# GpSimd takes the whole low-half subtraction in the two head attentions, VectorE makes both halves of their outputs

## What is computed

```python
qh = (q @ Wq).reshape(B, N, H, 8); kh, vh = the same of the context
attn = softmax(einsum(qh, kh) * 8 ** -0.5)      # 16 heads x 56 queries = 896 columns, 1500 keys
out = einsum(attn, vh).reshape(B, N, 128) @ Wo
x = x + out
```

## Time and profile before

| | us |
|---|---|
| median of 3 runs | 3920.25 (3919.48 to 3924.01) |
| the profiled execution's own time | 3916.58 |
| span of its trace | 3914.4 |
| first head, first to last start of L594 | 1222.8 to 1892.7 |
| second head, first to last start of L594 | 1973.6 to 2642.3 |

### The profile page before, as it was taken

The page is one execution under the profiler, slowest core; times in us unless marked ns, Lnnn a source line. Parts: engine busy times, 40 slices in busy tenths (PEclk is TensorE's granted clock), DMA queues, the critical chain, the costliest instruction groups (busy, mean ns, idle before and its releaser), DMA issues.

```text
span 3914.4 us, 126748 instructions
## 1 busy us (share of the span) xinstructions
PE 3608.5 (92%) x51275; PEld 2774.8 (71%) x51275; DVE 3262.6 (83%) x6773; ACT 2699.6 (69%) x5391; POOL 2060.1 (53%) x2087
## 2 busy tenths in 40 slices
PE   6999999989987999999799999996996999999987
PEld 4777777766654777777567777774774677777775
DVE  6988888858887999999799999987555888888863
ACT  4777777756655888888478888872442677777752
POOL 3666666668973555555545555661003444455451
PEclk7999999989998999999799999997997999999998
DMA  5333333215545555565166555530001212222100
GB/s 146 110 107 103 105 108 108 81 56 155 152 116 142 153 152 142 153 160 136 35 160 155 153 147 148 153 98 21 1 1 34 65 56 60 59 62 57 56 22 16
DMA packets 224592, 385.85 MB, mean 99 GB/s; under 512 B 71848, under 2 KB 127800, under 8 KB 222648
## 3 DMA queue, kind: packets, MB, share of 16 engines
q1 hardware_dynamic: 223560, 377.69, 35.5%
q10 hardware_dynamic: 448, 0.06, 0.0%
HBM read 252.30 MB, written 103.08 MB: 91 GB/s over the span
## 4 chain that ended last, share of the span: by engine, by line
PE 68%; DVE 17%; DMA 5%; issue 3%; SPq 3%; ACT 2%; POOL 1%; DVEq 0%; POOLq 0%; ACTq 0%
PE ps L208 64%; DVE wst L1177 5%; DMA big<-headq 4%; DVE wst L1160 2%; DVE wst L1157 2%; DVE relu L1157 1%; SPq L946 1%; DVE cTs L999 1%; DVE xn L188 1%; SPq L967 1%; PE ps L2006 1%; PE ps L712 1%; PE ps L275 1%; POOL wst L594 1%; ACT wst L1097 0%
## 5 line engine op out<-in xcount | busy, mean ns | idle before, releaser
L594 POOL TENSOR_TENSOR wst<-wst 125x448 bf16<-125x448 f32 (+2 forms) x1536 | 1356.6, 883 | 1235.5 <-ACT wst L792 639.5
L208 PEld LDWEIGHTS ps<-cx,wst 125*128 125x128 bf16 x32256 | 1196.2, 98 | 220.6 <-POOL wst L594 12.6
L208 PE MATMUL ps<-cx,wst 125*128 125x65 bf16 (+1 forms) x32256 | 1243.1, 193 | 10.5 <-POOL wst L594 9.3
L792 ACT ACTIVATE wst<-ps 125x448 f32<-125x448 f32 x1536 | 752.7, 544 | 275.2 <-PE ps L208 273.4
L1131 ACT ACTIVATE wst<-ps 125x448 f32<-125x448 f32 x1536 | 751.0, 544 | 93.1 <-PE ps L208 82.0
L208 PE MATMUL ps<-big,cx 128*125 128x448 bf16 (+1 forms) x3072 | 714.5, 354 | 0.9 <-DMA big<-topT 0.9
L848 DVE TENSOR_TENSOR wst<-wst 125x640 bf16<-125x640 f32 (+1 forms) x768 | 646.7, 842 | 21.9 <-ACT wst L792 21.7
L1177 DVE TENSOR_TENSOR wst<-wst 125x448 bf16<-125x448 f32 x768 | 627.1, 817 | 18.4 <-ACT wst L1131 18.1
L208 PE MATMUL ps<-big 97*128 97x224 bf16 (+2 forms) x3872 | 586.2, 280 | 5.5 <-POOL big L1430 2.1
L208 PEld LDWEIGHTS ps<-big,cx 128*125 128x125 bf16 (+1 forms) x3072 | 418.4, 137 | 142.2 <-DMA big<-topT 1.7
L208 PEld LDWEIGHTS ps<-big 97*128 97x128 bf16 (+2 forms) x3872 | 372.5, 98 | 183.9 <-ACT wst L1131 9.7
(11 more groups left out here) (268 smaller groups left out, 5232.6 us busy)
## 6 DMA issues: line engine op xcount, KB each, us to landing
big<-headk SPq DMA_DIRECT2D x192, 375.0 KB, 5.6
headk<-cTs SPq DMA_DIRECT2D x128, 375.0 KB, 4.6
cx<-ctxT SPq DMA_DIRECT2D x96, 375.0 KB, 10.0
cx<-ctxN SPq DMA_DIRECT2D x64, 377.9 KB
cx<-in_ctxN SPq DMA_DIRECT2D x64, 375.0 KB
big<-big SPq DMA_DIRECT2D x384, 56.0 KB, 2.6
big<-headq SPq DMA_DIRECT2D x64, 224.0 KB, 7.1
ctxN<-cx SPq DMA_DIRECT2D x32, 377.9 KB
```

What stands on the lines that cost most here:

```text
L208: return t.matmul(o, l, r, start=start, stop=stop, skip_group_check=True)
L594: g.tensor_tensor(pl[r][0:KP, at:], pf[r][0:KP, at:], pf[r][0:KP, at:].bitcast(BF16)[:, 1::2], ALU.subtract).then_inc(s["plp"], 1)
L792: e.activation(pf[T % 3][0:KP, cols], bank(2 + n2 % 3, 448)[0:KP], ACT.Exp, scale=scale).then_inc(s["ev"], 1)
```

## The change

In heads, `SPLIT` becomes 0: GpSimd subtracts all 896 columns in one instruction and VectorE none, and GpSimd no longer waits for `pl`. PE waits for GpSimd at block 0. The output of an image is made out of PSUM by VectorE alone, the high half in one instruction and the low half in seven of 64 columns (multiply by the reciprocal, subtract the high half). ScalarE's copy and GpSimd's subtraction for it go away in heads, and PE, before it writes an `acc` again, waits for both halves instead of for `raw`. Attentions 0 and 3 keep their split; only the counts that their semaphores wait for are renumbered.

```diff
--- before.py
+++ after.py
@@ -18,7 +18,7 @@
 NJ = HQ // 128
 HB = 16
 QB = 6
-SPLIT = (640, 448, 448, 512)
+SPLIT = (640, 0, 0, 512)
 NT = KT * B
 EPS = 1e-5
 TWICE = 6
@@ -589,12 +589,10 @@
                 if 0 <= T - 1 < NT:
                     r, at = (T - 1) % 3, SPLIT[ci]
                     w.wait_ge(s["ev"], evacuated(ci, T - 1) + 2)
-                    if ci in (1, 2):
-                        w.wait_ge(s["pl"], NT * ci + T)
                     g.tensor_tensor(pl[r][0:KP, at:], pf[r][0:KP, at:], pf[r][0:KP, at:].bitcast(BF16)[:, 1::2],
                                     ALU.subtract).then_inc(s["plp"], 1)
                     w.wait_ge(s["plp"], NT * ci + T)
-                if 0 <= (k := due(T, KT + 6)) < B - 1:
+                if 0 <= (k := due(T, KT + 6)) < (B - 1 if ci in (0, 3) else 0):
                     kb = B * ci + k
                     w.wait_ge(s["fp"], 2 * kb + 1)
                     g.tensor_tensor(O[:, k % HB, :, C:], raw[k % 2], O[:, k % HB, :, 0:C], ALU.subtract).then_inc(s["fp"], 1)
@@ -604,12 +602,13 @@
             k, i = divmod(T, KT)
             r, kb = T % 3, B * ci + k
             ph, o, of = pf[r][0:KP, :].bitcast(BF16)[:, 1::2], acc[k % 2], cnb[k % 3]
-            w.wait_ge(s["pl"], NT * ci + T + 1)
+            if SPLIT[ci]:
+                w.wait_ge(s["pl"], (NT if ci else 0) + T + 1)
             wait_values(w, ci, k)
             if kb >= 2:
-                w.wait_ge(s["fc"], kb - 1)
+                w.wait_ge(s["fp"], 2 * (kb - 1))
             for j in range(NJ):
-                if 128 * j == SPLIT[ci] or j == 3 and SPLIT[ci] == 448:
+                if 128 * j == SPLIT[ci]:
                     w.wait_ge(s["plp"], NT * ci + T + 1)
                 cols, at = slice(128 * j, 128 * j + 128), 65 * j
                 mm(t, o[:, at:at + 64], ph[:, cols], of[:, i, 65:129], i == 0 and j == 0, False)
@@ -625,6 +624,17 @@
             if k >= 2:
                 w.wait_ge(s["fp"], 2 * (kb - 1))
             w.wait_ge(s["rd"], kb + 1)
+            if not SPLIT[ci]:
+                if k >= HB:
+                    w.wait_ge(s["otr"], kb - HB + 1)
+                hi, lo = O[:, k % HB, :, 0:C], O[:, k % HB, :, C:]
+                v.tensor_tensor(hi, o[:, :, 0:C], per_row(rden[u][:, :], C), ALU.mult).then_inc(s["fp"], 1)
+                w.wait_ge(s["fp"], 2 * kb + 1)
+                for j in range(NJ):
+                    n = v.scalar_tensor_tensor(out=lo[:, j, :], in0=o[:, j, 0:C], scalar=rden[u][:, j:j + 1], in1=hi[:, j, :],
+                                               op0=ALU.mult, op1=ALU.subtract)
+                n.then_inc(s["fp"], 1)
+                return
             v.tensor_tensor(raw[u], o[:, :, 0:C], per_row(rden[u][:, :], C), ALU.mult).then_inc(s["fc"], 1)
             if k == B - 1:
                 w.wait_ge(s["fp"], 2 * kb + 1)
@@ -632,7 +642,7 @@
 
         def act_values(e, w, ci, k):
             kb = B * ci + k
-            w.wait_ge(s["fc"], kb + 1)
+            w.wait_ge(s["fc"], (B if ci else 0) + k + 1)
             w.wait_ge(s["fp"], 2 * kb)
             if k >= HB:
                 w.wait_ge(s["otr"], kb - HB + 1)
@@ -1105,8 +1115,6 @@
                     w.wait_ge(s[f"tops_{k % 2}"], 16 * (ci * B // 2 + k // 2))
                     e.activation(topT[k % 2][:, :], bank(2 + n2 % 3, 128)[0:NJ], ACT.Copy).then_inc(s["ev"], 1)
                     n2 += 1
-                if (k := due(T, KT + 4)) >= 0:
-                    act_values(e, w, ci, k)
                 what, p, k = head_slot(T)
                 if what == "keys split":
                     act_keys(e, w, ci, p, k)
@@ -1170,12 +1178,6 @@
             for c in range(3):
                 dve_keys(v, w, ci, 0, c)
             for T in range(-26, HEAD_LAST):
-                if 0 <= T - 1 < NT:
-                    r = (T - 1) % 3
-                    w.wait_ge(s["ev"], evacuated(ci, T - 1) + 1)
-                    to = SPLIT[ci]
-                    v.tensor_tensor(pl[r][0:KP, 0:to], pf[r][0:KP, 0:to], pf[r][0:KP, 0:to].bitcast(BF16)[:, 1::2],
-                                    ALU.subtract).then_inc(s["pl"], 1)
                 if (k := due(T, -18)) >= 0:
                     keys(k)
                 if (k := due(T, -5)) >= 0:
```

## The result

The changed kernel takes 3967.87 us (median of 4 runs, 3964.79 to 3968.99), the kernel before took 3919.86 in the same comparison (4 runs, 3918.67 to 3924.01): a ratio of 1.0115, 95% interval 1.0103 to 1.0127. It is slower by 48 us; 27 were forecast. The profiled execution took 3968.99.

What follows compares the result with a forecast made beforehand. The prediction took VectorE to set the heads' pace, about 1.75 us a step, passing to GpSimd at 1.757. Terms 7.2 + 1.0 + 11 + 4 + 4 = +27 us on 3920.25 gave 3947, range 3926 to 3984.

Steps and rivals of the forecast that it cites:

- the case that was held most likely: Heads: GpSimd sets the pace, with short dry spells; 3935 to 3965 us, chance 0.68.
- VectorE's pace passes to GpSimd's: Heads: the step goes from VectorE's 1.749 and 1.746 us to GpSimd's 1.757; +7.2 us.
- The dearer subtraction: Rival: GpSimd's 896-column subtraction takes 1.87 us, a step 1.95; +153 us, 4073, chance 0.05.
- The output's dry spell: PE's 16 output matmuls in two steps running make GpSimd stand 0.31 to 0.4 us, 30 times; +11 us.
- The transposed block: Its copy on ScalarE and a relu stand before the exponentials; GpSimd loses 0.12 us, 30 times; +4 us.
- The key difference: VectorE's L1165, once an image, waits for GpSimd, then holds its next subtraction 0.06 us, 62 times; +4 us.
- VectorE's block: Seven 64-column output instructions an image, 1.35 us, delay VectorE's next maximum by about 1.3 us; costed at nothing.
- The ends: Both ends of a head: last subtraction 0.75 us longer, first starts some 0.25 earlier; +1.0 us for two heads.
- The faster rival: Wide subtraction under 1.67 us, so PE sets the pace at 1.68 a step: 52 us less, 3868, chance 0.06.
- The costly exclusion: Rival: VectorE's key difference waits for GpSimd, the product is late; 1 us an image, +60, 3980, chance 0.07.

Runs made afterwards that it cites:

- The splits: Changed kernel with the outputs' low halves spread over four steps and VectorE given back 128 or 256 of 896 columns: 3945.45 and 3992.98 us.

## Why the prediction was right, and what it mis-sized

The time, 3967.87, lies 3 us above the 3935 to 3965 of the case that was held most likely, and inside the range of 3926 to 3984.

- *VectorE's pace passes to GpSimd's.* Right. L592 has a median of 1.682 us (1.679 forecast), 0.08 between two, 1.76 a step (1.757). Worth +9.6 us, +7.2 forecast; with a clear way in front of it (the kernel with more run-ahead and spread outputs) it gives 3935, and the kernel with GpSimd whole and the outputs before shows the same 1.76 without any dry spell. The dearer subtraction, 1.87 us at its bound, did not come; nor did the estimate by the Trainium skill's GPSIMD Engine Reference, section 3.1 (about 2.6 cycles an element, 1.94 us).
- *The output's dry spell*, 0.31 to 0.4 us: measured 0.35 us. Right, +10.
- *The transposed block*, 0.12 us: 0.09 as a rule, but up to 1.4 in four periods of the second head, mostly where the queries' transfer is late; +6 for +4. The prediction saw that transfer only as a ground for its costly rival.
- *The key difference*, 0.06 us: L592's longest is 1756 ns against 1680, about 0.07, as forecast +4. That it would wait up to 1.7 us for GpSimd was wrong here: its median is 410 ns, its longest 1884, and only 3 of 64 are over 600. At 1491.91 it starts just where GpSimd's step ends. With GpSimd at 768 columns the same instruction lasts 1594 ns in the mean.
- *VectorE's block*: this is the step that failed. It was costed at nothing because "PE's product meets it two slots (3.5 us) later". Its own length was right (1.35 us for the seven, 1.44 in the trace). But the reciprocal and the high half stand before them in the same block, so the maximum comes 2.0 us late (1485.7 to 1487.69), and most steps hold two products: the product that needs the bank is two products behind, which is one step. PE comes to it at 1487.1, 1.8 us after the product of 1485.30, not 3.5. It costs 0.55 us of GpSimd's time in 24 steps, 16 us by the starts of L592, and 21 us by the kernel that spreads it. The block alone is most of what the result has over the 27 forecast.
- *The ends*: +6.6 instead of +1.0. The first step starts 0.5 us later, not 0.25 earlier. From the last start of L592 to the last output's addition it is 11.0 us instead of 8.9 in the first head, 10.2 instead of 9.5 in the second. In the first head 0.75 of it is the longer subtraction, and nine more value matmuls wait for its end. Its last 32 matmuls also last 3.60 us instead of 3.27: the granted clock is 0.50 there (1.2 GHz), against 0.62 before. In the second head it is 0.65 there, and 0.50 before. PE had stood 0.94 us in front of each of the two steps of values before the clock fell. The remaining 3.3 us lie behind the second head, in stages that the change leaves as they were. From the last start of the second head to the end, the other kernels' traces scatter from 1270.8 to 1277.7 us, so it is not shown to be a cost of the change.

The sum, mended: 9.6 + 10 + 6 + 4 + 16 + 6.6 = 52, against 52.5 more of span. The mechanism forecast (GpSimd at its pace, with short dry spells) is what happened; the one term put at nothing was a third of the result.

*The faster rival* put its turn at 1.67 us and a gain of 52 us at a pace of 1.68. PE does reach 1.685, but only with a subtraction of 1.465 us and early queries; with the queries where they are, the gain at 1.465 is 9 us (0.3%), in a kernel that leaves work out. Another engine and a transfer stand close behind the one that is relieved.

*The costly exclusion*: in this change it had little to grip, since VectorE's large reading instruction is gone. The splits show it at full strength: 1.45 us for 128 columns. With GpSimd at 768 columns the key difference itself starts while GpSimd subtracts in 58 of 64 cases, and stands in each of them. By the Trainium skill's SBUF — State Buffer, section "SBUF: two separate sides", an operation of VectorE with two SBUF inputs and one of GpSimd that reads SBUF exclude each other for whole instructions, and the trace agrees: 1374 ns behind GpSimd's reading subtraction, 617 beside its MEMSET, with zeros in place of the subtraction.

## What to carry to other kernels

Giving one engine's share of a step wholly to another removes most of the lock between them, but makes that engine's longest instruction the pace; add up its duration and the gap behind it against the pace of before first, and then ask how many steps it holds in hand. A block that is made out of rare work on a nearly idle engine is not free: find the next result which that engine owes, and count from the first instruction of the block to it. And before a gain is booked on relieving an engine, look at what stands second in the chain of waits: here a transfer had 6.4% of the chain, and PE, once unheld, went at 1.685 us a step against 1.748.

## What the runs showed of the hardware

- GpSimd's subtraction from float32 and stride-2 bfloat16 lies on one line from 256 to 896 columns (256, 384, 448, 640, 768, 896): 612, 825, 932, 1252, 1465, 1680 ns at the least, that is 185 ns and 1.667 ns a column. Its MEMSET of 448 bfloat16 columns lasts 471 ns.
- VectorE's instruction with two SBUF inputs stands while GpSimd reads, so a smaller one gains little when GpSimd is busy. Its mean is 817 ns at 448 columns beside GpSimd's 448 (590 at the least), 857 at 256 beside 640 (412), 629 at 128 beside 768 (258). At 448 columns beside a GpSimd MEMSET it is not held: 617.
- Seven VectorE instructions of 64 columns out of PSUM take 1.44 us one behind the other, 277 ns each by their own length; their starts lie some 0.2 us apart. They have one input in PSUM and one in SBUF, and 139 of them ran wholly beside GpSimd's subtraction in 273 to 285 ns: they do not stand for it.
